# Batch statistics exchanged between the two partition halves by four 64x64 products into two PSUM banks, and an aggregate that reads both banks

## The chip, the cores and the metric

One core of one Trainium2 chip runs the kernel. The metric is the time of one execution in device microseconds (us); the times shown are of several executions, the profile is of one.

## The reference

Four stages are applied to an input of shape 8 x 64 x 16 x 16: two attention layers (L0, L1), a block of two batch-normalized 3x3 convolutions with one-bit weights (L2), and a whitening layer (L3). The change touches only the batch statistics of L2:

```
def batch_norm(x, gamma, beta):
    mean = jnp.mean(x, axis=(0, 2, 3), keepdims=True)
    var = jnp.mean((x - mean) ** 2, axis=(0, 2, 3), keepdims=True)
    xhat = (x - mean) * jax.lax.rsqrt(var + EPS)
    return xhat * gamma[None, :, None, None] + beta[None, :, None, None]
out = relu(batch_norm(x, gamma0, beta0))
out = conv3x3(out, quantize_w1bit(w0))
out = relu(batch_norm(out, gamma1, beta1))
out = conv3x3(out, quantize_w1bit(w1))
return out + x
```

## The kernel before

The 64 channels lie on the partitions twice: partitions 0 to 63 hold four of the eight images, partitions 64 to 127 the other four. A tile is therefore 128 partitions x 1024 columns: four pairs of images ("quarters" q = 0 to 3) of 256 columns each. Each engine has its own instruction list, written out by hand, and the engines are ordered by semaphores. Nothing reorders the lists.

The attention layers run from the start to about 40 us. Then L2 follows for n = 0 and n = 1, one batch norm and one convolution each:

1. VectorE makes six statistics per partition and quarter (bn_stats: L1104 for the first three quarters, L1169 for the last, and L1201 for n = 1). They lie in `stats[n]`, 128 x 24.
2. A channel's statistics are now on two partitions, c and c + 64. `combine` (L885) brings them together on TensorE. For each half g it multiplies `stats[n]` with a 128x128 selection matrix out of `kst`, which copies the rows of half g to both halves of the output. The two products lie side by side in one PSUM bank (`pb_small`, bank 3), so that each partition holds 48 numbers. `combine` is called twice for each n: on the first three quarters (18 columns) as soon as those are there, and on the last quarter (6 columns) after its statistics. The matrices are float32, and the trace shows two weight loads and two matmul records for each float32 product.
3. VectorE aggregates the 48 numbers to mean and variance (bn_aggr into `mv[n]`, L1205) and scales the first two quarters (`zn`, L1210). ScalarE makes the reciprocal deviation (`lnvar` L598, `rstd` L600) and then the convolution's input (`hi`, L610 and L607). VectorE makes its rest (`act`, `lo`, `hi`).
4. TensorE convolves: 144 products of 64x64 weights for each n (L910), fp16 in two parts, on diagonal and crosswise tiles of the array.

Around the second `combine`, TensorE's list is: `combine(1, quarters 0 to 2)`, `combine(1, quarter 3)`, nine 128x128 products that sum the convolution's weights (`pb_taps`, L974), eight filler products (`keep_warm`, L683), a wait for `zn`, one 128x128 product (L978), the convolution. On ScalarE the copy of that sum, `tap_all` (L596), stands ahead of `lnvar`. Around the first `combine` the list is: two calls of `combine`, two 128x1 products for the mean weight size (L959), twelve fillers (L683), the convolution.

After the second convolution come transposes (L935), a Gram matrix (L946), small products (L994, L996, L999) with a chain of small VectorE and GpSimd operations beside 30 fillers, and the final product (L1015), whose four 64x64 float32 products for each quarter lie on all four 64x64 tiles of the array. A product between 64 input partitions and 64 output partitions (`lanes(0)` or `lanes(1)`) is written 64*64 in the profile.

Of the kernel before, what the change touches and what calls it, by code (L numbers as in the profile page):

```python
# [14 lines left out]
F32 = mybir.dt.float32  # L15
# [7 lines left out]
P = 128  # L23
B, C, H, W = 8, 64, 16, 16
G = 2
PAIRS = B // G
N = H * W
# [14 lines left out]
HALF = 512  # L42
# [30 lines left out]
K_OWN = K_EPSN + Q * Q  # L73
# [44 lines left out]
def build(nc, x, attn_w, params, consts, select, conv_w, out):  # L118
    with ExitStack() as ctx:
        def sb(name, shape, dt=F32):  # L120
            return ctx.enter_context(nc.sbuf_tensor(name, shape, dt))

        def sem(name):
            return ctx.enter_context(nc.semaphore(name))
# [5 lines left out]
        kst = sb("kst", [P, K_COLS])  # L130
# [17 lines left out]
        stats = [sb(f"stats{n}", [P, 6 * k]) for n, k in ((0, PAIRS), (1, PAIRS))]  # L148
        mv = [sb(f"mv{n}", [P, 2]) for n in range(2)]
# [46 lines left out]
        final_w = sb("final_w", [P, Q, CJ])  # L196
        res = sb("res", [P, FREE])

        banks = [ctx.enter_context(nc.psum_tensor(f"bank{n}", [P, HALF], F32)) for n in range(8)]
        pb_rep, pb_v, pb_pv = banks[0], banks[1], banks[3]  # L200
        pb_rows = pb_v[:, N:2 * N]
        pb_s, pb_t = [banks[n] for n in (2, 4, 5)], banks[6:8]
# [1 line left out]
        pb_small = banks[3]  # L204
# [6 lines left out]
        pb_q = banks[1]  # L211
        pb_mean = banks[7]
        R_COL = 64
        pb_taps = banks[2][:, N:N + C]
        pb_pivot = banks[1][:, N:N + 1]
        pb_bias = banks[4]
        pb_means = banks[2]
# [27 lines left out]
        var_out, rstd_out = sem("var_out"), sem("rstd_out")  # L245
# [39 lines left out]
        def lanes(g):  # L285

            return slice(g * C, (g + 1) * C)

        def quarter(q):
            return slice(q * N, (q + 1) * N)  # L290
# [372 lines left out]
        def _(pe):  # L663
            mm = nc.tensor.matmul
# [216 lines left out]

            def combine(n, some):

                for g in range(G):
                    last = mm(pb_small[:, (PAIRS * g + some.start) * 6:(PAIRS * g + some.stop) * 6],  # L885
                              kst[:, K_OWN + g * P:K_OWN + (g + 1) * P],
                              stats[n][:, some.start * 6:some.stop * 6], start=True, stop=True)
                if some.stop == PAIRS:
                    last.then_inc(comb_mm, 1)

# [61 lines left out]
            pe.wait_ge(x_out, ITERS - 1)  # L952
            pe.wait_ge(stats0_out, PAIRS - 1)
            combine(0, range(PAIRS - 1))
            pe.wait_ge(last_stats, 1)
            combine(0, range(PAIRS - 1, PAIRS))
            pe.wait_ge(wabs_out, 2)
            for n in range(2):
                last = mm(pb_mean[:, n:n + 1], kst[:, K_ONES:K_ONES + P], wabs[n][:],  # L959
                          start=True, stop=True)  # L960
# [12 lines left out]
            for k in range(TAPS):  # L973
                last = mm(pb_taps, half[:, 0, :], taps[1][:, k, :], start=(k == 0), stop=(k == TAPS - 1))  # L974
# [4 lines left out]
               start=True, stop=False, skip_group_check=True)  # L979
# [5 lines left out]
            for g in range(G):  # L985
                last = mm(pb_pivot[lanes(g)], tap_all[lanes(0)], act_sum[lanes(0)], start=True, stop=True)
# [19 lines left out]
            for n, (k, first) in enumerate(PIECES):  # L1006
# [4 lines left out]
                for g in range(G):  # L1011
                    for half_out in range(2):
                        at = (k + half_out) * N + first

                        last = mm(pb_out[n][g][lanes(half_out), 0:P], weights[lanes(g)],  # L1015
                                  zc[lanes(g), at:at + P], start=True, stop=True)
# [3 lines left out]
        def _(dve):  # L1020
            ve = nc.vector
            steps = [0]

            def step(ins):

                ins.then_inc(dve_step, 1)
                steps[0] += 1
                dve.wait_ge(dve_step, steps[0])
# [3 lines left out]
            def power_of_two(n):  # L1032

                t, col = bn_t[n], (P_BNG0, P_BNG1)[n]
                step(ve.tensor_reduce(t[:, 0:1], prm[:, col:col + 2], AX.X, ALU.max, apply_absolute_value=True))
                step(ve.tensor_scalar(t[:, 1:2], t[:, 0:1], 1e-30, 1.0 / FP16_ROOM, ALU.max, ALU.mult))
                step(ve.tensor_scalar(t[:, 2:3].bitcast(U32), t[:, 1:2].bitcast(U32), 0x7F800000, None,
                                      ALU.bitwise_and))
                ve.reciprocal(t[:, 3:4], t[:, 2:3]).then_inc(pow2_out, 1)
                dve.wait_ge(pow2_out, n + 1)  # L1040
                step(ve.tensor_scalar(t[:, 4:6], prm[:, col:col + 2], t[:, 3:4], None, ALU.mult))
# [136 lines left out]
            def first_line(n, q):  # L1178

                ve.tensor_scalar(act32[:, quarter(q)], zn[n][:, q], rstd[n][:], bn_t[n][:, 5:6],  # L1180
                                 ALU.mult, ALU.add).then_inc(line_out, 1)

            def first_low(n, q):

                dve.wait_ge(line_out, 2 * n + q + 1)
                dve.wait_ge(hi_act, 2 * n + q + 1)
                ve.scalar_tensor_tensor(flat(lo, n, q), act32[:, quarter(q)], 0.0, flat(hi, n, q),
                                        ALU.max, ALU.subtract).then_inc(lo_out, 1)

            def later_inputs(n, q):  # L1190

                dve.wait_ge(act_out, 2 * n + q - 1)
                ve.tensor_copy(flat(hi, n, q), act32[:, quarter(q)]).then_inc(hi_dve, 1)  # L1193
                dve.wait_ge(hi_dve, 2 * n + q - 1)
                ve.tensor_tensor(flat(lo, n, q), act32[:, quarter(q)], flat(hi, n, q),
                                 ALU.subtract).then_inc(lo_out, 1)

            def conv0_statistics(q):

                dve.wait_ge(conv_mm, q + 1)  # L1200
                ve.bn_stats(stats[1][:, 6 * q:6 * q + 6], pb_conv[0][q][:, 0:N]).then_inc(stats_out, 1)  # L1201

            for n in range(2):
                dve.wait_ge(comb_mm, n + 1)
                ve.bn_aggr(mv[n][:], pb_small[:, 0:2 * 6 * PAIRS]).then_inc(var_out, 1)  # L1205
                dve.wait_ge(var_out, n + 1)
                t = bn_t[n]
                for q in range(2):
                    src = xs[LAYERS][:, quarter(q)] if n == 0 else pb_conv[0][q][:, 0:N]
                    ve.tensor_scalar(zn[n][:, q], src, mv[n][:, 0:1], t[:, 4:5], ALU.subtract,  # L1210
                                     ALU.mult).then_inc(z_out, 1)
                dve.wait_ge(rstd_out, n + 1)
                dve.wait_ge(z_out, 2 * n + 2)
                first_line(n, 0)
                if n == 0:
                    first_line(0, 1)
                    first_low(0, 0)
                    first_low(0, 1)
                    dve.wait_ge(e_mm, 1)
                    step(ve.tensor_copy(emean[:], pb_mean[:, 0:2]))  # L1220
                    step(ve.tensor_tensor(esq[:], emean[:, 0:1], emean[:, 0:1], ALU.mult))
                    step(ve.tensor_scalar(esq[:], esq[:], E_SQUARE_MIN, None, ALU.max))
                    later_inputs(0, 2)
                    step(ve.reciprocal(einv[:], esq[:]))
                    later_inputs(0, 3)
                    power_of_two(1)
                    conv0_statistics(0)
                    step(ve.tensor_scalar(eps1[:], einv[:], BN_EPS * PAIRS * N, None, ALU.mult))
                    dve.wait_ge(stats_out, 1)
                    ve.tensor_tensor(stats[1][:, M2:M2 + 1], stats[1][:, M2:M2 + 1], eps1[:],  # L1230
                                     ALU.add).then_inc(eps1_set, 1)
                    conv0_statistics(1)
                    ve.tensor_scalar(nscale[:], emean[:, 1:2], -1.0 / N, None, ALU.mult).then_inc(pivot_set, 1)
                    ve.tensor_scalar(nxm[:], mv[0][:, 0:1], -1.0, None, ALU.mult).then_inc(pivot_set, 1)
                    conv0_statistics(2)
                    conv0_statistics(3)
                else:
                    first_low(1, 0)
                    first_line(1, 1)
                    first_low(1, 1)  # L1240
                    for q in range(2, PAIRS):
                        later_inputs(1, q)
# [32 lines left out]
            def products(j):  # L1275

                left, cols = Q - 1 - j, 2 * Q - 1 - j
                row = tt[:, j:j + 1, j + 1:].to_broadcast([P, left, cols])
                lij = tt[:, j, j + 1:Q].unsqueeze(2).to_broadcast([P, left, cols])
                return tt[:, j + 1:, j + 1:], upd[:, j + 1:, j + 1:], row, lij  # L1280

            below, some, row, lij = products(0)
# [3 lines left out]
            for j in range(1, Q - 1):  # L1286
                below, some, row, lij = products(j)
# [89 lines left out]
```

## Time and profile before

| What | Value |
|---|---|
| Time, median of 3 runs | 69.2 us (69.17 to 69.22) |
| Time of the profiled execution | 69.05 us |
| Its span, first to last instruction | 67.3 us |
| TensorE busy | 57.7 us, 86% of the span |
| VectorE busy | 48.0 us, 71% |
| ScalarE busy | 42.5 us, 63% |
| GpSimd busy | 20.0 us, 30% |
| `combine` on the chain that ended last | 3% of the span |

The span is what the trace covers. The execution's own time is 1.75 us longer, for what lies before the first and after the last instruction. A row of the timeline that merges several instructions (xN) gives the first start and the time until the last end; the mean of one instruction is in the view by groups. A weight load (PEld) and a matmul (PE) are separate records, and they overlap.

### The profile page before, as it was taken

What the parts mean: (1) busy time and instruction counts of PE and PEld (TensorE: products, weight loads), DVE (VectorE), ACT (ScalarE), POOL (GpSimd) and SP (SyncE); (2) the same over time, 40 slices, a digit from 0 to 9 for tenths busy, and PEclk for the clock granted to TensorE, in tenths of its full rate; (3) what the DMA queues carried; (4) which work ended last, traced back from release to release, by engine and by line L of the source; (5) the groups of instructions that cost most, each with busy time, mean ns of one, the idle gap of its engine ahead of it and who ended that gap; (6) DMA issues with size and microseconds to landing.
All of it is one profiled execution on the core that took longest, in us unless ns stands there. A gap on an engine that the chain in (4) does not pass through costs nothing. (4 is left out here: it accounts for less than half of the span.)

```text
span 67.3 us, 2133 instructions
## 1 busy us (share of the span) xinstructions
PE 57.7 (86%) x795; PEld 36.7 (54%) x795; DVE 48.0 (71%) x133; ACT 42.5 (63%) x137; POOL 20.0 (30%) x58
## 2 busy tenths in 40 slices
PE   5994898889899989958998989999499999999910
PEld 3323433655465627432553758698385997855500
DVE  0079899595949899994946775988949978575530
ACT  0711098999997699789998663930028564167630
POOL 5000955530554608680303040301303050045000
PEclk9999999999999999999999999999999999999999
DMA  0998930000000000000000000000000000000044
GB/s 0 254 245 205 370 151 0 0 0 10 0 0 5 0 0 0 0 19 0 0 0 0 0 0 10 0 0 10 0 0 0 10 0 0 10 0 0 0 166 146
DMA packets 2457, 2.71 MB, mean 40 GB/s; under 512 B 400, under 2 KB 2064, under 8 KB 2448
## 3 DMA queue, kind: packets, MB, share of 16 engines
q1 hardware_dynamic: 2160, 2.39, 11.5%
q10 hardware_dynamic: 288, 0.20, 0.9%
q8 instruction: 6, 0.10, 0.5%
q14 instruction: 3, 0.02, 0.1%
HBM read 2.06 MB, written 0.52 MB: 38 GB/s over the span
## 5 line engine op out<-in xcount | busy, mean ns | idle before, releaser
L507 ACT ACTIVATE bank<-bank,negmax 128x256 f32<-128x256 f32 x32 | 14.5, 457 | 1.7 <-DVE negmax L1054 1.7
L683 PE MATMUL bank<-const-bfloat16-1.0 128*64 128x512 bf16 x82 | 11.5, 418 | 0.8 <-PEq L1362 0.8
L1054 DVE TENSOR_REDUCE negmax<-bank 128x2 f32<-128x512 f32 x16 | 10.5, 685 | 1.9 <-PE bank L742 1.8
L527 ACT ACTIVATE probs<-bank 128x512 f32<-128x512 f32 x16 | 8.8, 602 | 1.1 <-PE bank L766 1.1
L805 PE MATMUL bank<-probs,vt 128*64 128x256 f32 x64 | 8.5, 386 | 0.3 <-DVE cut L1064 0.3
L910 PE MATMUL bank<-hi,taps 64*64 64x225 f16 (+2 forms) x144 | 6.9, 267 | 0.1
L683 PEld LDWEIGHTS bank<-const-bfloat16-1.0 128*64 128x64 bf16 x82 | 4.7, 117 | 4.2 <-issue 1.6
L507 ACT ACTIVATION_READ_ACCUMULATOR bank<-bank,negmax 128x1 f32 x32 | 6.9, 216 | 0.0
L910 PE MATMUL bank<-lo,taps 64*64 64x225 f16 (+2 forms) x144 | 6.9, 266 | 0.0
L360 POOL TENSOR_TENSOR cut<-cut 64x256 f32<-64x256 f32 x7 | 4.3, 610 | 8.3 <-DVE cut L1064 5.3
L910 PEld LDWEIGHTS bank<-hi,taps 64*64 64x64 bf16 x144 | 5.8, 107 | 0.9 <-issue 0.4
L910 PEld LDWEIGHTS bank<-lo,taps 64*64 64x64 bf16 x144 | 6.2, 107 | 0.0
L805 PEld LDWEIGHTS bank<-probs,vt 128*64 128x64 f32 x64 | 5.1, 136 | 1.5 <-issue 0.8
L694 PE MATMUL bank<-x,aw 128*64 128x256 f32 x32 | 5.2, 421 | 0.1
L1081 DVE CAST qk<-bank 128x512 bf16<-128x512 f32 x7 | 4.8, 684 | 0.5 <-PE bank L710 0.5
L376 POOL TENSOR_TENSOR shift<-negmax,lntot 128x4 f32<-128x4 f32 x8 | 1.6, 203 | 10.8 <-issue 9.5
L710 PE MATMUL bank<-cut,half 128*64 128x256 bf16 x32 | 3.4, 284 | 1.5 <-DVE cut L1073 1.0
L367 POOL TENSOR_TENSOR cut<-cut 32x256 f32<-32x256 f32 x7 | 4.3, 610 | 0.5
L1087 DVE COPY vt<-bank 128x256 f32<-128x256 f32 x8 | 3.4, 422 | 1.4 <-PE bank L726 1.4
L1064 DVE TENSOR_SCALAR cut<-bank,prm 128x256 f32<-128x256 f32 x8 | 3.9, 482 | 0.6 <-PE bank L694 0.5
L535 ACT ACTIVATE shift_t<-bank 128x256 bf16<-128x256 f32 x8 | 3.1, 385 | 1.3 <-PE bank L781 1.2
L596 ACT ACTIVATE tap_all<-bank 128x64 f32<-128x64 f32 x1 | 0.2, 223 | 5.7 <-PE bank L974 5.7
(134 smaller groups left out, 103.3 us busy)
## 6 DMA issues: line engine op xcount, KB each, us to landing
cw<-conv_w SPq DMA_DIRECT2D x2, 288.0 KB, 4.2
x<-x_in SPq DMA_DIRECT2D x4, 128.0 KB, 2.6
out<-res SPq DMA_DIRECT2D x4, 128.0 KB, 1.8
kst<-consts SPq DMA_DIRECT2D x1, 428.0 KB, 4.9
aw<-attn_w ACTq DMA_DIRECT2D x1, 128.0 KB, 2.5
aw<-attn_w SPq DMA_DIRECT2D x1, 128.0 KB, 3.0
half<-select SPq DMA_DIRECT2D x1, 96.0 KB, 2.7
kst<-consts SPq DMA_DIRECT2D x1, 64.5 KB, 3.4
```

The lines of the kernel that those rows point to most:

```text
L360: nc.gpsimd.tensor_tensor(some, some, tops(some), ALU.subtract).then_inc(part1_out, 1)
L367: nc.gpsimd.tensor_tensor(some, some, tops(some), ALU.subtract).then_inc(part2_out, 1)
L507: nc.scalar.activation(part, part, ACT.Exp, bias=negmax[:, i % 2, n:n + 1], accum_out=total[:, i % 2, n:n + 1]).then_inc(total_out, 1)
L527: nc.scalar.activation(probs[:, i % 2, g], pb_t[g][:].rearrange("p (t n) -> p t n", t=CH), ACT.Exp).then_inc(exp_out, 1)
L683: mm(bank[lanes(h)], filler[:, lanes(h)], filled, start=True, stop=True)
L694: last = mm(proj(i)[lanes(h)], aw[:, w + h * C:w + (h + 1) * C], x_of(i), start=True, stop=True)
L710: last = mm(to, half[:, 1 + o, lanes(h)], tops(cut[:, i]), start=True, stop=True)
L805: last = mm(mixed(i)[g * C:(g + 1) * C], vt[:, i % 2, t, g * C:(g + 1) * C], probs[:, i % 2, g, t, :], start=(t == 0 and i < ITERS - 1), s ...
L910: last = mm(img(pb_conv[n][q][lanes(to), 0:N])[:, kept(dy, H), kept(dx, W)], taps[n][lanes(g), tap, :], (hi, lo)[part][n][lanes(g), q, shi ...
L1054: ve.tensor_reduce(negmax[:, i % 2, g * CH:(g + 1) * CH], pb_s[(2 * i + g) % 3][:].rearrange("p (t n) -> p t n", t=CH), AX.X, ALU.max, neg ...
L1064: ve.tensor_scalar(cut[:, i], proj(i), prm[:, bias:bias + 1], None, ALU.add).then_inc(part0_out, 1)
L1081: ve.tensor_copy(qk[:, i].rearrange("p o n -> p (o n)"), pb_rep[:]).then_inc(qk_out, 1)
```

## The change

`combine` issues four 64x64 products in place of two 128x128 products. The first two copy each half's statistics to the same half of bank 3 (tile rows and columns 0-0 and 1-1). The other two copy each half's statistics to the opposite half of bank 2 (0-1 and 1-0). Banks 2 and 3 become one tensor `both`, 128 x 2 x 512, and the aggregate reads 24 columns of each. As bank 2 now holds statistics, the weight sum `pb_taps` moves from bank 2 to bank 7.

```
+        both = ctx.enter_context(nc.psum_tensor("both", [P, 2, HALF], F32))
+        banks = [both[:, n - 2] if n in (2, 3) else
+                 ctx.enter_context(nc.psum_tensor(f"bank{n}", [P, HALF], F32)) for n in range(8)]
+        GROUPS = 6 * PAIRS
...
-        pb_taps = banks[2][:, N:N + C]
+        pb_taps = banks[7][:, N:N + C]
...
             def combine(n, some):
-                for g in range(G):
-                    last = mm(pb_small[:, (PAIRS * g + some.start) * 6:(PAIRS * g + some.stop) * 6],
-                              kst[:, K_OWN + g * P:K_OWN + (g + 1) * P],
-                              stats[n][:, some.start * 6:some.stop * 6], start=True, stop=True)
+                cols = slice(some.start * 6, some.stop * 6)
+                for other in range(2):
+                    for g in range(G):
+                        h = 1 - g if other else g
+                        own = K_OWN + g * P + h * C
+                        last = mm(both[lanes(h), 1 - other, cols], kst[lanes(g), own:own + C],
+                                  stats[n][lanes(g), cols], start=True, stop=True)
                 if some.stop == PAIRS:
                     last.then_inc(comb_mm, 1)
...
-                ve.bn_aggr(mv[n][:], pb_small[:, 0:2 * 6 * PAIRS]).then_inc(var_out, 1)
+                ve.bn_aggr(mv[n][:], both[:, :, 0:GROUPS]).then_inc(var_out, 1)
```

## Rows read from the trace of the kernel before

**Rows 1.** The page: span, busy digits of TensorE in 40 slices, and its granted clock.
```profile
span 67.3 us, 2133 instructions
PE   5994898889899989958998989999499999999910
PEclk9999999999999999999999999999999999999999
```

**Rows 2.** The chain that ended last: start, length (us) and what.
```profile
39.56 0.44 DVE stats L1104
40.00 0.14 issue
40.13 1.06 PE bank L885 x8
...
41.31 0.39 DVE mv L1205
...
48.17 0.35 DVE stats L1201
48.52 0.14 issue
48.66 1.04 PE bank L885 x8
...
49.72 0.39 DVE mv L1205
...
50.77 0.61 ACT hi L610
```

**Rows 3.** The timeline around both combines: start, length (us), engine, line, operation.
```profile
40.09 0.42 DVE L1169 BATCH_NORM_STATS2 stats<-bank 128x6 f32<-128x256 f32 x1
40.10 0.98 PEld L885 LDWEIGHTS bank<-stats,kst 128*128 128x128 f32 x8 [0.69 <-issue]
47.28 0.47 PE L910 MATMUL bank<-lo,taps 64*64 64x225 f16 x6
48.09 0.76 DVE L1201 BATCH_NORM_STATS2 stats<-bank 128x6 f32<-128x256 f32 x2
48.63 0.97 PEld L885 LDWEIGHTS bank<-stats,kst 128*128 128x128 f32 x8 [1.13 <-DVE stats L1230]
48.66 1.03 PE L885 MATMUL bank<-stats,kst 128*128 128x18 f32 x8 [0.90 <-DVE stats L1201]
```

**Rows 4.** The line of combine: durations (min/median/max ns) of its loads and matmuls.
```profile
L885 PEld LDWEIGHTS bank<-stats,kst x16: 186/191/192, 40.1 to 49.4; 128*128 128x128 f32 x16
L885 PE MATMUL bank<-stats,kst x16: 254/256/268, 40.1 to 49.4; 128*128 128x18 f32 x8, 128*128 128x6 f32 x8
```

**Rows 5.** The timeline of the last quarter's final product, on four 64x64 tiles.
```profile
63.70 0.24 PEld L1015 LDWEIGHTS bank<-zc,final_w 64*64 64x64 f32 x8 [0.37 <-issue]
63.73 0.45 PE L1015 MATMUL bank<-zc,final_w 64*64 64x128 f32 x8 [0.16 <-DVE res L1308]
```

**Rows 6.** The line of the final product: durations of 64x64 float32 loads and matmuls.
```profile
L1015 PEld LDWEIGHTS bank<-zc,final_w x32: 129/133/133, 62.7 to 63.8; 64*64 64x64 f32 x32
L1015 PE MATMUL bank<-zc,final_w x32: 269/269/320, 62.7 to 63.9; 64*64 64x128 f32 x32
```

**Rows 7.** The timeline of L986, two float32 products from one half of the rows.
```profile
53.24 0.13 PEld L986 LDWEIGHTS bank<-act_sum,tap_all 64*64 64x64 f32 x1
53.30 0.13 PEld L986 LDWEIGHTS bank<-act_sum,tap_all 64*64 64x64 f32 x1
53.34 0.13 PEld L986 LDWEIGHTS bank<-act_sum,tap_all 64*64 64x64 f32 x1
53.40 0.13 PEld L986 LDWEIGHTS bank<-act_sum,tap_all 64*64 64x64 f32 x1
53.43 0.19 PE L986 MATMUL bank<-act_sum,tap_all 64*64 64x1 f32 x1
```

**Rows 8.** Groups by line of VectorE: two shapes of a 512-column read.
```profile
L1054 DVE TENSOR_REDUCE negmax<-bank 128x2 f32<-128x512 f32 x16 | 10.5, 685 | 1.9 <-PE bank L742 1.8
L1081 DVE CAST qk<-bank 128x512 bf16<-128x512 f32 x7 | 4.8, 684 | 0.5 <-PE bank L710 0.5
```

**Rows 9.** The timeline where TensorE changes from 64*64 to 128*128.
```profile
55.49 0.58 PE L910 MATMUL bank<-lo,taps 64*64 64x240 f16 x7
55.99 0.31 PEld L935 LDWEIGHTS bank<-kst,yc 128*128 128x128 f32 x3 [0.18 <-issue]
```

**Rows 10.** The timeline behind the second combine.
```profile
49.43 0.41 PEld L974 LDWEIGHTS bank<-taps,half 128*128 128x128 f16 x9
49.54 0.42 PE L974 MATMUL bank<-taps,half 128*128 128x64 bf16 x9
49.90 1.06 PE L683 MATMUL bank<-const-bfloat16-1.0 128*64 128x512 bf16 x8
50.00 0.22 ACT L596 ACTIVATE tap_all<-bank 128x64 f32<-128x64 f32 x1 [5.68 <-PE bank L974]
50.13 0.20 ACT L598 ACTIVATE lnvar<-mv 128x1 f32<-128x1 f32 x1
50.37 0.20 ACT L600 ACTIVATE rstd<-lnvar 128x1 f32<-128x1 f32 x1
50.88 0.30 PEld L978 LDWEIGHTS bank<-kst 128*128 128x128 f32 x2 [0.41 <-DVE zn L1210]
51.43 0.93 PEld L910 LDWEIGHTS bank<-hi,taps 64*64 64x64 bf16 x26 [0.25 <-ACT hi L610]
```

More of the change, by code:

```diff
@@ L197, in build @@
         res = sb("res", [P, FREE])
-        banks = [ctx.enter_context(nc.psum_tensor(f"bank{n}", [P, HALF], F32)) for n in range(8)]
+        both = ctx.enter_context(nc.psum_tensor("both", [P, 2, HALF], F32))
+        banks = [both[:, n - 2] if n in (2, 3) else
+                 ctx.enter_context(nc.psum_tensor(f"bank{n}", [P, HALF], F32)) for n in range(8)]
+        GROUPS = 6 * PAIRS
         pb_rep, pb_v, pb_pv = banks[0], banks[1], banks[3]
```

## The prediction

> **What bounds the kernel now.** I read the page first. TensorE is busy in nearly every slice and its clock is granted in full throughout [rows 1], so a share of busy time decides nothing here. The question is which wait ends last at each `combine`. The chain that ended last answers it [rows 2]. Both calls of `combine` lie on it: VectorE's statistics, then eight TensorE passes (1.06 us at n = 0, 1.04 us at n = 1), then the aggregate `mv`. VectorE does nothing else meanwhile, so the end of `combine` sets the start of the aggregate at 41.31 and at 49.72.
>
> The timeline shows how much of the 1.04 us counts [rows 3]. The second call, on the last quarter, is what VectorE waits for. At n = 0 the last statistics end at 40.09 + 0.42 = 40.51. The eight loads start at 40.10 and take 0.98 us to the last end. One load takes 0.191 [rows 4], so they follow each other every (0.98 - 0.19) / 7 = 0.11 us. The fifth load, the first of the second call, starts at 40.10 + 4 x 0.11, plus a little, about 40.56. This is 0.05 after the statistics. At n = 1 the last statistics end at 48.09 + 0.76 = 48.85, but the fifth load starts only at 48.63 + 0.44 = 49.07, as the first call's four passes stand ahead of it. From that fifth load to the last matmul's end it is 41.17 (40.13 + 1.04, or 1.06 by the chain) - 40.56 = 0.61 at n = 0, and 48.66 + 1.03 - 49.07 = 0.62 at n = 1. In steps: three pitches of 0.11, 0.03 from load to matmul, and one matmul of 0.256 [rows 4], together 0.62.
>
> **The change, part by part.** Each call of `combine` goes from four passes on the whole array (two products, two passes each) to eight passes on quarter tiles. What counts is how eight such passes pack. Two places of the trace show it.
>
> The nearest row is the final product: four 64x64 float32 products on the same four tiles, eight passes, started on an idle array [rows 5]. The eight loads take 0.24 us in all, at 0.133 each [rows 6], so they start within 0.11 us, one every 0.016: the tiles load side by side. From the first load to the last matmul's end it is 63.73 + 0.45 - 63.70 = 0.48. These move 128 columns, where the changed call moves 18 or 6, so 0.48 is the upper end. The lower end is the other place: two 64x64 float32 products with one column, from one half of the rows [rows 7]. Their four loads start every 0.053 and the last matmul ends at 53.62, 0.38 after the first load. Each half of the rows gets exactly four such passes in the new call, so with the halves side by side this is a direct model of it. I take the middle, 0.43.
>
> *Release.* At a wait on an idle TensorE the load starts 0.11 after VectorE's end (48.52 to 48.63 [rows 2, 3]); at n = 0 it was 0.05. I take 0.08, and 0.05 to 0.11 as its bounds. The first call's eight passes start at 40.10 and 48.63 as before, load within 0.11 to 0.16, and are out of the way before either release.
>
> *n = 0:* the second call ends at 40.51 + 0.08 + 0.43 = 41.02, against 41.17: 0.15 earlier (bounds 0.07 to 0.23).
>
> *n = 1:* it ends at 48.85 + 0.08 + 0.43 = 49.36, against 49.69: 0.33 earlier (0.25 to 0.41). Here the release also stops waiting for the first call.
>
> *The aggregate* reads 48 numbers as before, but as 2 x 24 from two banks. No row has a read across banks. The nearest pair: a reduction over 512 columns in two runs takes 0.685, a flat cast of 512 columns 0.684 [rows 8]; so a run boundary costs nothing. I take 0, bounds 0 to 0.05 for each of the two. Less than nothing is excluded, since the count of elements is unchanged.
>
> *Does the gain at n = 0 survive the first convolution?* From `mv` at 41.31 the chain is VectorE with one operation behind the other up to the statistics of n = 1. TensorE's last matmul there ends at 47.28 + 0.47 = 47.75 [rows 3], while VectorE's statistics of the third and fourth quarter start only at 48.09 [rows 3]: 0.3 us of cover. The convolution, ScalarE and GpSimd take their inputs from `mv`'s followers and move with them. So the 0.15 passes in full.
>
> *What is late next behind n = 1.* TensorE changes its tile shape between `combine` and the weight sum (L974), which it didn't before. The trace shows such a change [rows 9]: the last 64*64 matmul ends at 56.07, the first 128*128 load starts at 55.99, which is 0.08 before that end. With equal shapes the load of L974 started at 49.43, 0.26 before combine's end of 49.69. So L974's loads start at 49.36 - 0.08 = 49.28, 0.15 earlier than before, not 0.33. It and the fillers are queued there, and ScalarE's `tap_all` waits for it, ahead of `lnvar`. `tap_all` starts 0.15 to 0.25 earlier (its first matmul no longer stands 0.11 behind its load [rows 10]), that is at 49.75 to 49.85; `lnvar` follows 0.13 later, and `rstd` ends 0.44 after that start, at 50.32 to 50.42. ScalarE's `hi` waits for `zn` as well, and this lets it go at 50.77 - 0.33 = 50.44. So the late copy is just hidden; if the drain costs 0.1 more it takes that much from the gain. I charge 0.03. The fillers end at 50.96 and L978's load starts 0.08 before it, at 50.88 [rows 10]: it follows them by 0.15 to 0.25, still before the convolution needs the array at 51.43 - 0.30 = 51.13. At n = 0 the same change of shape delays L959 and the fillers, and the convolution starts some 0.1 later than it could; the 0.3 of cover takes this.
>
> A rule of the Trainium skill speaks against the change here: TensorEngine Tiling (Array Packing), Key Properties, says that changing the tiling mode, and not just the tile, drains TensorE. The trace agrees, as the load at 55.99 waits for nearly the whole last matmul; by the page alone, without a row for its price, the delay would stay unknown, and by the row it is what is worked out above.
>
> *The second convolution* (51.43 to 56.07) and all behind it hang on `hi`: the transposes, the last fillers and the final product have no event at a fixed time. They shift as a whole. The move of `pb_taps` to bank 7 costs nothing: its readers are ahead of the convolution that writes that bank.
>
> *Sum:* 0.15 + 0.33 - 0.03 = 0.45 us. The profiled execution would go from 69.05 to 68.60, and against the median of 69.20 the forecast is 68.75. Its own range, from the bounds (0.07 + 0.25 - 0.10 for a dearer drain = 0.22, and 0.23 + 0.41 = 0.64), is 68.56 to 68.98.
>
> **The rivals.**
>
> *A: only the diagonal pairs run side by side, and the packing of four fails.* The new order is 0-0, 1-1, 0-1, 1-0, while the final product's is row by row. If 0-1 has to wait for both passes of 0-0 in the same rows, a call has four slots of 0.11 as before: 0.62, and nothing is won at either n. Time 69.2. For it: the loads of [rows 7] follow each other at 0.053 within one half of the rows. Against it: eight loads start in 0.11 [rows 5], four of them in each half of the rows, and even 0.053 a load gives a call of 0.45. The Trainium skill has a rule of this kind: TensorE: Matmul & The Clock Gate, The mechanism (packing small matmuls), says that weight loads overlap matmuls in flight only when the row group differs. By it this case is what happens; the trace disagrees, as all eight loads of [rows 5] start before the first matmul ends.
>
> *B: slower. The passes don't overlap at all,* each taking the 0.11 slot that a pass of today takes. Then a call costs 0.88 + 0.29. At n = 0 the second call's last matmul ends at 40.10 + 15 x 0.11 + 0.29 = 42.04 (+0.87), at n = 1 at 50.57 (+0.88): 70.95. The point that decides is the pitch: at n = 1, 48.63 + 15p + 0.29 = 49.69 gives p = 0.051, at n = 0 40.56 + 7p + 0.29 = 41.17 gives 0.046. Above it the change loses. The loads of the final product came every 0.016 [rows 5].
>
> *C: the read across two banks is dear.* From 0.22 each it eats the whole gain: 69.2 and above. Nothing in the trace speaks for it, and nothing measures it.
>
> *D: one of the two gains is hidden anyway,* by the weight sum ahead of `lnvar` or by the convolution: 0.15 to 0.3 is left, 68.9 to 69.05.
>
> **How the numbers follow.** A measurement of this kernel tells 0.2%, 0.14 us, from no change. Forecast 0.65, D 0.13, A 0.11, B 0.05, C 0.06 (half at no change, half slower). Faster is the forecast and D, less 0.02 for the part of D within 0.14: 0.76. The same is A, half of C and that rest: 0.16, of which I move 0.01 to slower for what I overlook: 0.15. Slower is B, half of C and that: 0.09. For eight in ten the range runs from 68.50 (0.06 beyond the forecast's own range, 0.05 left out below) to 69.20, which leaves B, most of C and half of A out above, 0.15.
>
> **What the profile of the changed kernel would show.** Right: 32 passes at the line of `combine`, 16 for each n, with loads of 0.13; the aggregate about 0.15 earlier at n = 0 and 0.48 earlier at n = 1 (0.15 + 0.33) at an unchanged 376 ns; the second convolution 0.45 earlier. The prediction is wrong if the second call takes 0.6 us or more from its first load, if the aggregate takes longer, or if `hi` of n = 1 waits for `rstd` and not for `zn`.

## The result and the profile after

| | before | changed |
|---|---|---|
| Time, median | 69.20 us | 68.35 us |
| Ratio, 95% interval | | 0.9879 (0.986 to 0.9899) |
| `combine`: passes for each n | 8 | 16 |
| Last statistics' end to aggregate's start, n = 0 | 0.80 us | 0.51 us |
| The same, n = 1 | 0.87 us | 0.42 us |

By the ratio the change makes the kernel 1.2% faster, which is 0.84 us with an interval of 0.70 to 0.97. I forecast 0.45, and a range of times from 68.50 to 69.20. The sign and the place were right, the size was not, and the time lies outside the range. Timed a second time (e1 below) it was 0.71 us faster.

The profiled execution of the changed kernel took 69.81 us and was one of its slower ones, while every time and ratio in this document is of the fast ones (68.31 to 68.36 here). In it the last statistics of the attention layers ended 1.47 us later than in the profile before (41.98 against 40.51), so only stretches within L2 are set beside those of before here. The chain that ended last, start and length in us, of the changed kernel:

```profile
41.65 0.33 DVE stats L1175
41.99 0.04 issue
42.03 0.34 PE both L892 x8
...
42.49 0.39 DVE mv L1211
...
49.35 0.35 DVE stats L1207
49.70 0.14 issue
49.84 0.58 PE both L892 x16
...
50.44 0.39 DVE mv L1211
...
51.49 0.61 ACT hi L613
```

These answer to [rows 2]. At n = 0 the chain no longer passes through all of `combine`: the early call is off it, and only the last quarter's eight passes, 0.34 us, lie between the statistics and the aggregate. At n = 1 sixteen passes take 0.58 where eight took 1.04. The aggregate's length is unchanged at 0.39.

The timeline of the same kernel shows the second call at each n:

```profile
41.56 0.42 DVE L1175 BATCH_NORM_STATS2 stats<-bank 128x6 f32<-128x256 f32 x1
42.03 0.21 PEld L892 LDWEIGHTS both<-stats,kst 64*64 64x64 f32 x8 [0.22 <-DVE stats L1175]
42.03 0.30 PE L892 MATMUL both<-stats,kst 64*64 64x6 f32 x8
42.26 0.52 PEld L965 LDWEIGHTS bank<-wabs,kst 128*128 128x128 f32 x4
...
49.27 0.75 DVE L1207 BATCH_NORM_STATS2 stats<-bank 128x6 f32<-128x256 f32 x2
...
50.08 0.30 PE L892 MATMUL both<-stats,kst 64*64 64x6 f32 x8
50.30 0.32 PEld L980 LDWEIGHTS bank<-taps,half 128*128 128x128 f16 x9
50.44 0.38 DVE L1211 BATCH_NORM_AGGREGATE mv<-both 128x2 f32<-128x48 f32 x1 [0.42 <-PE both L892]
50.78 0.22 ACT L599 ACTIVATE tap_all<-bank 128x64 f32<-128x64 f32 x1 [5.27 <-PE bank L980]
50.90 0.20 ACT L601 ACTIVATE lnvar<-mv 128x1 f32<-128x1 f32 x1
51.49 0.60 ACT L613 ACTIVATE hi<-zn,bn_t,rstd 128x256 f16<-128x256 f32 x1 [0.17 <-DVE zn L1216]
```

The statistics end at 41.56 + 0.42 = 41.98 and at 49.27 + 0.75 = 50.02. The second call starts 0.05 later at n = 0 and 0.06 later at n = 1, and takes 0.30 us from its first load to the last matmul's end both times. I had forecast 0.08 and 0.43. The fifth load of [rows 3] started 0.05 and 0.22 after the statistics, and 0.62 of call followed.

The durations by line, to set beside [rows 4] and [rows 6] (min/median/max ns):

```profile
L892 PEld LDWEIGHTS both<-stats,kst x32: 129/131/133, 41.6 to 50.2; 64*64 64x64 f32 x32
L892 PE MATMUL both<-stats,kst x32: 197/208/229, 41.6 to 50.2; 64*64 64x18 f32 x16, 64*64 64x6 f32 x16
```

The two lines mix both calls; by shape, a matmul of 6 columns lasts 0.208 us on the new tile, where it lasted 0.256 before, and one of 128 columns in the final product 0.269 (the median of [rows 6]). This is the first hint at why the call is shorter than forecast.

The rest of L2 is the same length. From the first aggregate to the last statistics' end it was 48.85 - 41.31 = 7.54 and is 50.02 - 42.49 = 7.53; from the second aggregate to the second convolution's first load it was 1.71 and is 1.71 (52.15 - 50.44); from there to the end of the span it was 15.9 and is 15.9. So the two waits, 0.29 and 0.45, are the whole difference, 0.74 us.

### The profile page after: what moved, and what is told of

It reads as the page before. It is cut to its first block and busy times, and to the rows that moved or that the text cites. A ratio compares the mean times of both kernels' runs of the same rounds, so it can differ in the third digit from the quotient of the medians.

```text
span 68.0 us, 2165 instructions
## 1 busy us (share of the span) xinstructions
PE 59.0 (87%) x811; PEld 36.5 (54%) x811; DVE 47.9 (70%) x133; ACT 42.5 (63%) x137; POOL 20.0 (29%) x58
## 5 line engine op out<-in xcount | busy, mean ns | idle before, releaser
L686 PE MATMUL bank<-const-bfloat16-1.0 128*64 128x512 bf16 x64 | 9.2, 429 | 0.8 <-PEq L1368 0.8
L510 ACT ACTIVATE bank<-bank,negmax 128x256 f32<-128x256 f32 x20 | 9.1, 460 | 0.2 <-DVE negmax L1060 0.2
L808 PE MATMUL both<-probs,vt 128*64 128x256 f32 x56 | 7.6, 387 | 0.3 <-issue 0.3
L1060 DVE TENSOR_REDUCE negmax<-bank 128x2 f32<-128x512 f32 x10 | 6.7, 685 | 1.4 <-PE bank L745 0.8
L510 ACT ACTIVATE both<-both,negmax 128x256 f32<-128x256 f32 x12 | 5.4, 451 | 2.6 <-DVE negmax L1060 2.6
L686 PEld LDWEIGHTS bank<-const-bfloat16-1.0 128*64 128x64 bf16 x64 | 3.7, 119 | 3.7 <-issue 1.6
L808 PEld LDWEIGHTS both<-probs,vt 128*64 128x64 f32 x56 | 4.4, 136 | 1.4 <-issue 0.8
L1060 DVE TENSOR_REDUCE negmax<-both 128x2 f32<-128x512 f32 x6 | 4.1, 683 | 1.1 <-PE bank L745 1.1
L697 PE MATMUL both<-x,aw 128*64 128x256 f32 x24 | 4.8, 484 | 0.1
L510 ACT ACTIVATION_READ_ACCUMULATOR bank<-bank,negmax 128x1 f32 x20 | 4.4, 219 | 0.0
```

The lines of the kernel that those rows point to most:

```text
L510: nc.scalar.activation(part, part, ACT.Exp, bias=negmax[:, i % 2, n:n + 1], accum_out=total[:, i % 2, n:n + 1]).then_inc(total_out, 1)
L686: mm(bank[lanes(h)], filler[:, lanes(h)], filled, start=True, stop=True)
L697: last = mm(proj(i)[lanes(h)], aw[:, w + h * C:w + (h + 1) * C], x_of(i), start=True, stop=True)
L808: last = mm(mixed(i)[g * C:(g + 1) * C], vt[:, i % 2, t, g * C:(g + 1) * C], probs[:, i % 2, g, t, :], start=(t == 0 and i < ITERS - 1), s ...
L1060: ve.tensor_reduce(negmax[:, i % 2, g * CH:(g + 1) * CH], pb_s[(2 * i + g) % 3][:].rearrange("p (t n) -> p t n", t=CH), AX.X, ALU.max, neg ...
```

## The experiments

Each was timed in alternation with the kernel before, on one chip for each group of four. "Against before" is the difference, in us, of the medians of the runs that the ratio compares. The ratio is estimated for itself and can differ from the quotient of the medians: for e10 and e11 it means 0.84 and 0.11 us less time, not 0.79 and 0.05. Times are compared within a group: e1, e5, e7, e8; e2, e3, e4, e9; e6, e10, e11, e12. The waits are those of the table above.

| Run | wait n = 0 | wait n = 1 | time | against before | ratio (interval) |
|---|---|---|---|---|---|
| e1, changed kernel again | 0.52 | 0.42 | 68.42 | -0.71 | 0.9895 (0.9874 to 0.9915) |
| e5, second call moves 128 columns | 0.67 | 0.57 | 68.69 | -0.44 | 0.9929 (0.9908 to 0.9949) |
| e7, n = 0 only | 0.52 | 0.88 | 68.82 | -0.31 | 0.9957 (0.9942 to 0.9973) |
| e8, n = 1 only | 0.80 | 0.42 | 68.71 | -0.42 | 0.9935 (0.9906 to 0.9964) |
| e2, row order | 0.52 | 0.42 | 68.44 | -0.75 | 0.9891 (0.9873 to 0.9909) |
| e3, two 64x128 products | 0.58 | 0.49 | 68.66 | -0.53 | 0.9916 (0.9901 to 0.9932) |
| e4, four 128x64 products | 0.60 | 0.51 | 68.62 | -0.57 | 0.9915 (0.9894 to 0.9937) |
| e9, changed, one call | 0.61 | 0.53 | 68.72 | -0.47 | 0.9922 (0.9901 to 0.9943) |
| e6, before, one call | 0.88 | 0.78 | 69.16 | +0.02 | 1.0001 (0.9985 to 1.0016) |
| e10, half of the rows | 0.48 | 0.38 | 68.35 | -0.79 | 0.9879 (0.9847 to 0.9911) |
| e11, one tile | 0.81 | 0.72 | 69.09 | -0.05 | 0.9984 (0.9971 to 0.9997) |
| e12, scale operations early | 0.52 | 0.42 | 68.07 | -1.07 | 0.9844 (0.9825 to 0.9863) |

**e1: the changed kernel again.** No edit.

> The changed kernel once more, for a profile to set beside the one of before. Theory T (the gain is all in the two waits for combine): from the last statistics' end to the aggregate's start it is about 0.51 us at n = 0 (0.80 before) and 0.42 us at n = 1 (0.87 before), 0.29 + 0.45 = 0.74 us, and every other stretch, the attention layers above all, agrees with before within 0.05 us, so the time is 68.45. Rival R (part of the gain comes from the attention layers, whose banks 2 and 3 have moved in PSUM): the stretch up to the last statistics is shorter by 0.1 us or more, and the time is 68.35.

```profile
40.20 0.42 DVE L1175 BATCH_NORM_STATS2 stats<-bank 128x6 f32<-128x256 f32 x1
...
41.14 0.38 DVE L1211 BATCH_NORM_AGGREGATE mv<-both 128x2 f32<-128x48 f32 x1 [0.52 <-PE both L892]
41.44 1.49 PE L686 MATMUL bank<-const-bfloat16-1.0 128*64 128x512 bf16 x12
...
47.92 0.75 DVE L1207 BATCH_NORM_STATS2 stats<-bank 128x6 f32<-128x256 f32 x2
...
49.09 0.38 DVE L1211 BATCH_NORM_AGGREGATE mv<-both 128x2 f32<-128x48 f32 x1 [0.42 <-PE both L892]
```

The last statistics of the attention layers end at 40.62, 0.11 later than before (40.51), not 0.1 or more earlier, so rival R falls. T had put that stretch within 0.05 of before, which it is not; what made it longer in this execution stays open. That profiled execution took 68.42 us against 69.05 before: the two waits less 0.11. The median fell by 0.71. The waits' 0.74 lies between this and the first measurement's 0.84, and inside both intervals, so nothing else has to be explained.

**e7 and e8: one n alone.** e7 keeps the four products for n = 0, e8 for n = 1 (there the condition is `n == 1`). The other n gets:

```
+                if n == 0:
...
+                else:
+                    for g in range(G):
+                        last = mm(both[:, g, cols], kst[:, K_OWN + g * P:K_OWN + (g + 1) * P],
+                                  stats[n][:, cols], start=True, stop=True)
```

> Only n = 0 uses the four 64x64 products; n = 1 uses two 128x128 products, one into each bank. Theory T (the two gains stand each by itself and pass to the end in full): the first aggregate starts 0.29 us earlier, the second keeps its 0.87 us of wait, and the time is 0.29 below the kernel before, 68.9. Rival R (the first convolution takes up a part of it): the stretch from the first aggregate to the last statistics of n = 1 grows over its 7.53 us, and the time is 0.1 to 0.2 below.

> Only n = 1 uses the four 64x64 products; n = 0 uses two 128x128 products, one into each bank. Theory T: the second aggregate starts 0.45 us earlier against its statistics, the time is 0.45 below the kernel before, 68.75, and this gain and that of the other half add up to that of the whole change. Rival R (the weight sum, late by the change of tile shape, holds back what follows): the stretch from the second aggregate to the second convolution grows over 1.71 us and the time is 0.3 below or less.

The gains were 0.31 and 0.42, together 0.73, which is e1's 0.71. Each wait changed only where its `combine` was changed, as the table's e7 and e8 show. Neither the first convolution nor the weight sum takes anything back: in e7 it is 7.53 us from the first aggregate to the last statistics' end, and in e8 1.70 from the second aggregate to the convolution, as before. Theory T holds at both places. These kernels also read both banks behind 128x128 products, with a wait of 0.80 and 0.88 as before: the two banks cost nothing and give nothing.

**e5: the second call moves 128 columns.** `stats` is 128 columns wider, with zeros in them.

```
-                cols = slice(some.start * 6, some.stop * 6)
+                cols = slice(some.start * 6, some.stop * 6 if some.stop < PAIRS else some.start * 6 + 128)
```

> As changed, but the second call of each combine moves 128 columns in place of 6 (the columns past the last quarter's are zeros that nobody reads). Theory T (my 0.43 us for a call was too long because it was taken from products of 128 columns, and with 6 columns neither the move nor the array's exit takes that long): the second call takes 0.45 to 0.48 us from its first load to its last matmul's end against 0.30, both aggregates start 0.15 to 0.18 later, and the time is 0.3 to 0.36 above the changed kernel's. Rival R (the tile shape alone makes the call short, the columns don't matter): the call stays at 0.30 to 0.33 and the time within 0.06 of the changed kernel's.

The groups by line and form, busy us and mean ns:

```profile
L895 PE MATMUL both<-stats,kst 64*64 64x128 f32 x16 | 0.9, 295 | 0.0
L895 PE MATMUL both<-stats,kst 64*64 64x18 f32 x16 | 0.6, 214 | 1.3 <-DVE stats L1211 0.9 <-DVE stats L1114 0.4
```

The timeline of both calls at n = 0, and the chain:

```profile
40.38 0.77 PE L895 MATMUL both<-stats,kst 64*64 64x18 f32 x16 [0.37 <-DVE stats L1114]
```

```profile
40.70 0.49 PE both L895 x8
...
41.32 0.39 DVE mv L1215
```

The second call's first load starts at 40.70 and its last matmul ends at 40.38 + 0.77 = 41.15, so the call takes 0.45 us where it took 0.30. Both waits grew by 0.15, and so did the chain's piece of the second call, from 0.34 to 0.49. The time grew by 0.27, a little less than the 0.3 to 0.36 that T gave. The 0.45 is nearly the 0.48 of [rows 5]: the row that I took for the upper end was about right for 128 columns, and 0.18 too long for 6.

**e10: half of the rows.** Only tiles 0-0 and 0-1, so the kernel leaves out the statistics of the second half:

```
+                for h in range(2):
+                    own = K_OWN + h * C
+                    last = mm(both[lanes(h), 1 - h, cols], kst[lanes(0), own:own + C],
+                              stats[n][lanes(0), cols], start=True, stop=True)
```

> Only the two products of tiles 0-0 and 0-1, both from the first half of the rows, four passes on an idle array (the second half's statistics are left out). Theory T (the 0.38 us of the trace's two products from one half of the rows was due to the convolution's passes between them, not to the half): a call takes 0.28 to 0.32 us, as long as the one with four tiles, and the waits stay at 0.51 and 0.42. Rival U (one half of the rows takes one load every 0.053 us also when alone): three pitches, so 0.16 + 0.03 + 0.21 = 0.40 us.

```profile
40.00 0.42 DVE L1173 BATCH_NORM_STATS2 stats<-bank 128x6 f32<-128x256 f32 x1
...
40.04 0.71 PE L890 MATMUL both<-stats,kst 64*64 64x18 f32 x8 [0.27 <-DVE stats L1108]
40.47 0.19 PEld L890 LDWEIGHTS both<-stats,kst 64*64 64x64 f32 x4 [0.23 <-DVE stats L1173]
40.90 0.38 DVE L1209 BATCH_NORM_AGGREGATE mv<-both 128x2 f32<-128x48 f32 x1 [0.48 <-PE both L890]
```

In the timeline four loads take 0.19 in all, so they start every (0.19 - 0.13) / 3 = 0.02 us, not every 0.053 as in [rows 7]. The matmuls end at 40.04 + 0.71 = 40.75, 0.28 after the first load at 40.47. That falls on T's 0.28 to 0.32 and not on U's 0.40. The 0.38 that I took for the lower end belongs to two products whose loads stand between those of the convolution. Also, half the passes save only 0.04 of each wait: with the tiles side by side, the number of passes hardly sets the call's length.

**e2: order row by row.**

```
-                for other in range(2):
-                    for g in range(G):
-                        h = 1 - g if other else g
-                        own = K_OWN + g * P + h * C
-                        last = mm(both[lanes(h), 1 - other, cols], kst[lanes(g), own:own + C],
+                for g in range(G):
+                    for h in range(2):
+                        own = K_OWN + g * P + h * C
+                        last = mm(both[lanes(h), int(g == h), cols], kst[lanes(g), own:own + C],
```

> The same four 64x64 products, issued row by row (0-0, 0-1, 1-0, 1-1) as in the final product, the same banks. Theory T (each of the four tiles takes its loads and matmuls by itself, whatever the order): a call stays at 0.30 to 0.34 us, the time within 0.05 of the changed kernel's 68.43. Rival A (tiles of one half of the rows hold each other up, so the order that alternates between the halves is what makes the call short): the second call grows by 0.05 to 0.11 us at each n, and the time by 0.1 to 0.2.

The waits are those of e1, 0.52 and 0.42, and the gain (0.75 us, e1's is 0.71) is the same within the intervals: the order doesn't matter, rival A's mechanism is absent.

**e3 and e4: two tiles in place of four.** e3 has two 64x128 products (one for each half of the rows), e4 four 128x64 products (column tiles, contracting over all rows):

```
# e3
+                for g in range(G):
+                    last = mm(both[:, g, cols], kst[lanes(g), K_OWN + g * P:K_OWN + (g + 1) * P],
+                              stats[n][lanes(g), cols], start=True, stop=True)
# e4
+                for g in range(G):
+                    for h in range(2):
+                        own = K_OWN + g * P + h * C
+                        last = mm(both[lanes(h), int(g == h), cols], kst[:, own:own + C],
+                                  stats[n][:, cols], start=True, stop=True)
```

> Two 64x128 products for each call, one from each half of the rows, into one bank each; the aggregate as changed. Four passes, two tiles. Theory T (what shortens the call is that the passes of different tiles load side by side, and then only half the passes need a slot of 0.11): two slots, 0.11 + 0.03 + 0.21 to 0.26 = 0.35 to 0.40 us for a call against 0.30 to 0.34, the time 0.05 to 0.15 above the changed kernel's. Rival S (the shortness is that of 64 columns of weights, loads of 0.13 against 0.19): a call of 0.45 or more and at least 0.25 above.

> Four 128x64 products for each call, contracting over all 128 rows, on two column tiles, into the same banks. Eight passes, four to a tile. Theory T: the Gram matrix's passes of this shape follow each other every (1.15 - 0.23) / 31 = 0.03 us, so a call takes 7 x 0.03 + 0.03 + 0.25 = 0.49 us, and the time is 0.3 to 0.4 above the changed kernel's. Rival S (64 columns of weights are enough): a call of 0.35 or less and at most 0.1 above.

The groups by line and form of e3 and then of e4, and for both the chain's piece of the second call at n = 0:

```profile
L889 PE MATMUL both<-stats,kst 64*128 64x6 f32 x8 | 0.8, 261 | 0.0
...
40.57 0.41 PE both L889 x4
```

```profile
L891 PE MATMUL both<-stats,kst 128*64 128x6 f32 x16 | 0.8, 205 | 0.0
...
42.11 0.43 PE both L891 x8
```

e3's call takes 0.39 us (40.57 to 40.96), within T's 0.35 to 0.40. Its waits are 0.06 and 0.07 longer than the changed kernel's, 0.13 in all, as T expected. Its time is 0.22 above that of e2, which stands in for the changed kernel on this chip; this is more than the 0.15 at most that T gave, and no trace shows where the rest lies. S's 0.25 and a call of 0.45 or more are not reached. e4 fits neither theory: 0.18 above e2, and 0.17 by the waits, where T expected 0.3 to 0.4 and S at most 0.1. Its call took 0.40 us (42.10 to 42.50), or 0.43 by the chain, and not T's 0.49: a matmul lasted 0.205 where T put 0.25, and the eight loads took 0.32 in all, one every 0.026 where T put 0.03. By the waits (1.67 before, 0.94 with four tiles, 1.07 and 1.11 with two) two tiles give about four fifths of the gain, and four the rest. The two shapes also show what goes with the length of one matmul with few columns: 0.205 and 0.208 where the tile has 64 output columns (e4 and the changed kernel), 0.261 and 0.256 where it has 128 (e3 and before), whatever the rows.

**e11: one tile.** The second call is made of one product of tile 0-0, four times over. The early call keeps the four tiles. The kernel leaves out part of the statistics. The edit of the second call:

```
+                            last = mm(both[lanes(0), 1, GROUPS - 6:GROUPS], kst[lanes(0), K_OWN:K_OWN + C],
+                                      stats[n][lanes(0), GROUPS - 6:GROUPS], start=True, stop=True)
```

> The last quarter's call is four times the product of tile 0-0, eight passes one behind the other on one tile; the early call is four products of 24 columns made of the first quarter's statistics (so the results of the other quarters are left out). Theory T (what makes the changed call short is that four tiles work at once): the passes follow each other every 0.05 to 0.11 us, the call takes 0.6 to 1.0 us against 0.30, each wait grows by 0.3 to 0.7, and the time is 69.0 to 69.8, at or above the kernel before. Rival V (passes with so few columns are short wherever they lie): a call of 0.4 or less, the time within 0.2 of the changed kernel's.

```profile
40.44 0.42 DVE L1180 BATCH_NORM_STATS2 stats<-bank 128x6 f32<-128x256 f32 x1
...
40.91 0.54 PEld L897 LDWEIGHTS both<-stats,kst 64*64 64x64 f32 x8 [0.22 <-DVE stats L1180]
40.91 0.63 PE L897 MATMUL both<-stats,kst 64*64 64x6 f32 x8
41.67 0.38 DVE L1216 BATCH_NORM_AGGREGATE mv<-both 128x2 f32<-128x48 f32 x1 [0.81 <-PE both L897]
```

On one tile the loads start every (0.54 - 0.13) / 7 = 0.058 us and the call takes 0.63, twice the four tiles' 0.30. The time is nearly that of the kernel before: 0.05 less by the medians, 0.11 (0.02 to 0.20) by the ratio, 0.14 by the waits. The packing is what pays: the same number of passes of the same shape, in a row, gives nothing at n = 0 (0.81 against 0.80) and 0.15 at n = 1, where the short early call is out of the way. This is also the mechanism of rival B, measured for the second call. It costs 0.058 a pass and not the 0.11 with which I priced it at 70.95; that the early call's passes go in a row as well was not run.

**e6 and e9: one call for each n.** The early call is left out, and the last call takes all 24 columns:

```
-            combine(1, range(PAIRS - 1))
             pe.wait_ge(stats_out, PAIRS)
-            combine(1, range(PAIRS - 1, PAIRS))
+            combine(1, range(PAIRS))
```

> The kernel before with one call of combine for each n, on all 24 columns, after the last statistics: four passes on the whole array. Theory T (of the 0.45 us won at n = 1, about 0.16 is that the last quarter's call no longer queues behind the early one): at n = 1 the wait from the last statistics to the aggregate falls from 0.87 to 0.11 + 0.62 + 0.03 = 0.76 us, at n = 0 it grows from 0.80 to 0.86, and the time is 0.05 below the kernel before. Rival Q (the queue costs nothing, the whole difference is the packing): the wait at n = 1 is 0.87 or more, and the time 0.05 to 0.1 above.

> As changed, but one call of combine for each n, on all 24 columns, after the last statistics. Theory T (the early call is no longer ahead of anything): the wait from the last statistics to the aggregate is 0.05 to 0.1 longer at n = 0 and at n = 1, as the load now waits 0.11 and not 0.05 after them on an idle array and the matmuls move 24 columns and not 6; the time is 0.1 to 0.2 above the changed kernel's. Rival Q (at n = 1 the early call still stands in the way, 16 passes in a row): the wait at n = 1 is 0.05 shorter or more.

In the kernel before (e6) the wait at n = 1 fell from 0.87 to 0.78, at n = 0 it grew from 0.80 to 0.88, as T expected within 0.02; the time was within its interval of T's -0.05 and of no change. So the early call with four whole-array passes cost 0.09 at n = 1, though its purpose was to save, and it saved 0.08 at n = 0. In the changed kernel (e9) leaving it out costs at both places, 0.09 and 0.11, and 0.28 in time against e2, where T expected 0.1 to 0.2. With short calls the early one is out of the way. Without it the load waits 0.11 and 0.12 after the statistics instead of 0.05 and 0.06, and the call with 24 columns takes 0.34 instead of 0.30. Rival Q is wrong in both kernels.

**e12: the scale operations early.**

```
             statistics(0)
+            power_of_two(1)
...
                     later_inputs(0, 3)
-                    power_of_two(1)
                     conv0_statistics(0)
```

> The changed kernel with the five scale operations of the second batch norm (0.9 us of VectorE in the first convolution) moved into VectorE's idle time in the attention layers, behind the first quarter's statistics. Theory T (VectorE alone sets the end of the first convolution, and TensorE has 0.3 us of cover on the third quarter's statistics, as the prediction said): TensorE becomes the bound, 0.4 to 0.6 of the 0.9 us are won, and the time is 67.8 to 68.0. Rival W (the convolution is the bound already): less than 0.15 is won.

The chain between the two aggregates:

```profile
41.54 1.43 PE bank L686 x12
42.96 2.80 PE bank L916 x84
45.76 0.04 issue
45.80 2.10 PE bank L916 x43
47.90 0.02 issue
47.92 0.44 DVE stats L1208
48.36 0.04 issue
48.41 0.34 PE both L892 x8
```

The time fell to 68.07, 1.07 (1.6%) below the kernel before, 0.36 more than e1's gain: this is the fastest version here. T's mechanism shows, at slightly less than its 0.4 to 0.6. From the first aggregate to the last statistics' end it is now 48.35 - 41.17 = 7.18 us, where it was 7.53. Of the 0.9 us taken off VectorE about 0.36 is won, then the chain runs through TensorE, from the twelve fillers straight into the convolution. In the changed kernel itself this path had been covered by VectorE. Whether fewer fillers there give more was not tried.

## Why the prediction was wrong in size

**What bounds the kernel: right.** Both `combine` calls were on the chain, VectorE was idle beside them, and all that was won there came out at the end (e7 and e8 add up to e1).

**The length of a call: this step failed.** I took "the middle, 0.43" of 0.38 and 0.48; it is 0.30. Both ends were rows of other conditions. The 0.48 of the final product [rows 5] holds the passage of 128 columns; e5 gives the changed call 128 columns and its length rises by 0.15, to 0.45. The 0.38 of [rows 7] was measured with the convolution's passes in between; e10 runs two tiles of one half of the rows without them and takes 0.28. In steps: the eight loads take 0.21 in all, so the last starts 0.21 - 0.13 = 0.08 after the first, and the last matmul, of 0.208, ends 0.22 after that. I had seen that 6 columns are fewer than 128, and named 0.48 the upper end for it, but I didn't take the 128 columns' time off. The step cost 0.13 at each n, 0.26 in the sum.

**The release: 0.05 to 0.06 at both places, not 0.08.** The 0.11 holds for an idle array (early calls, e6, e9); behind an early call it is shorter. 0.05 in the sum. That at n = 1 the second call no longer queues was forecast and shows: its load starts 0.06 and not 0.22 after the statistics. In e6, where the queue is gone and the load starts 0.11 after them, the wait is 0.09 shorter.

**The change of tile shape: right in the row, without effect.** L965's load starts at 42.26, before the last matmul's end at 42.33, as in [rows 9]; L980's at 50.30 before 50.38. With equal shapes the next load had started 0.26 before that end, now it is 0.07 and 0.08. The Trainium skill, TensorEngine Tiling (Array Packing), Key Properties, says that a change of the tiling mode drains TensorE. The trace agrees in the main, as the load waits for most of the last matmul. As the call ended earlier than forecast, `tap_all` came 50.78 - 50.02 = 0.76 after the statistics (1.15 before), 0.39 earlier. `lnvar` starts 0.46 behind the aggregate's start where it was 0.41, so the copy does delay it by 0.05, and `hi` still waits for `zn`, 1.05 behind the aggregate as before. In e6, where the copy starts 0.26 after the aggregate's start, `lnvar` still comes 0.41 after it. The 0.03 that I charged is 0.

The sum as measured: 0.45 + 0.26 + 0.05 + 0.03 = 0.79, against 0.74 by the waits. The missing 0.05 lies between the last matmul's end and the aggregate's start: 0.16 and 0.06 us, against 0.14 and 0.03 before. Matmul ends are modelled in the profile, and no run settles this.

**The aggregate over two banks: right,** 376 ns as before, and rival C is excluded with it. The two rows behind this step [rows 8] compared different operations and were thin evidence; the 0 to 0.05 that I allowed for each aggregate was also left out of my own range. **The first convolution takes nothing back: right,** 7.53 against 7.54. The cover of 0.3 us on TensorE was stated about right too: with VectorE relieved of 0.9, about 0.36 was won before TensorE took over (e12).

**The rivals.** A is excluded by e2, and by e10, which shows that two tiles in the same rows load side by side. The Trainium skill's rule behind A, in TensorE: Matmul & The Clock Gate, The mechanism, is that weight loads overlap matmuls in flight only when the row group differs. In e10 all four loads start within 0.06 us while a matmul lasts 0.21, and all have the same rows, and in e11 even loads on one and the same tile start every 0.058 while a matmul lasts 0.20; the measurement goes against that rule in this case. The same section also allows the overlap for a load into the background weight buffer, and no trace here shows whether these loads were of that kind. B's loads in a row were seen only where the products share a tile (e11), and cost less than I priced. D did not happen. The range was too narrow since its lower end was built from the same two rows: 0.30 lies outside the bounds of 0.38 and 0.48.

## What to carry to other kernels

A short product on the critical path costs its latency, not its work: splitting it over all four 64x64 tiles halved the time from its first load to its last result (0.62 to 0.30 us) although the number of passes doubled, while the same passes on one tile took 0.63. Take the price of such a call from rows with the same number of moved columns and with an array as idle, or take the difference off. And look at what an early, partial call blocks: with long passes it stood in the way of the one that mattered at n = 1 (0.09 us, e6), with short ones it helped at both places (e9).

## What the runs showed of the hardware

The length of a float32 matmul with few moved columns followed the output columns of its tile and not its rows: 0.256 (128x128) and 0.261 (64x128) against 0.205 (128x64) and 0.208 (64x64), each with 6 columns. With 128 moved columns the 64x64 one takes 0.295 in e5 and a median of 0.269 in the final product. Loads of 64 float32 weight columns start every 0.011 us over four tiles ((0.21 - 0.13) / 7), 0.02 over two tiles in one half of the rows, 0.026 over two column tiles of 128 rows, and 0.058 on one tile.
